# One core, fused attention and feed-forward over 64 sequences: the pieces of the software pipeline put in another order

## What is computed

```python
# layer 0: cross attention to 77 context tokens, 16 heads of 8
scores = einsum('bhqd,bhkd->bhqk', q, k) / sqrt(8)
scores = clip(0.5 * scores * mask + 0.5 * scores, -50, 50)
x = layernorm(x + softmax(scores) @ v @ Wo + bo) * gamma + beta
# layer 1: self attention, 16 heads of 64, rotary, causal within segments of 64 tokens,
# every query also sees 16 equal memory keys and 16 persistent keys
xn = rms_norm(x);  q, k, v = split(xn @ to_qkv_w);  q, k = rope(q), rope(k)
x = x + softmax(q @ [k_mem, k_pm, k].T / 8, masked) @ [v_mem, pm, v] @ to_out_w
a, g = split(rms_norm(x) @ ff_w1 + ff_b1);  x = x + silu(g) * a @ ff_w2 + ff_b2
```

## Time and profile before

| | us |
|---|---|
| median of 3 runs (lowest to highest) | 1216.44 (1213.78 to 1217.11) |
| profiled execution, its own time | 1214.23 |
| its span, first to last instruction | 1212.4 |
| busy: PE / PE weight loads / DVE / ACT / POOL | 1163.1 / 1019.5 / 987.0 / 1009.3 / 993.7 |
| mean granted TensorE clock, share of full | 0.996 |

### The profile page before, as it was taken

How to read it: one execution, slowest core, us unless ns; L and a number is a source line. 1 busy time by engine, 2 the same in 40 slices (tenths; PEclk the granted TensorE clock), 3 DMA queues, 4 the chain that set the end, 5 groups by cost and what they waited for, 6 DMA issues and landing times.

```text
span 1212.4 us, 54784 instructions
## 1 busy us (share of the span) xinstructions
PE 1163.1 (96%) x20707; PEld 1019.5 (84%) x20707; DVE 987.0 (81%) x2574; ACT 1009.3 (83%) x3341; POOL 993.7 (82%) x1678
## 2 busy tenths in 40 slices
PE   3799999999999999999999999999999999999985
PEld 2588888888888888888888888888888888888874
DVE  5578888888888888888888888888888888888872
ACT  1488888888888888888888888888888888888874
POOL 1578988888888888888888888888888888888874
PEclk9999999999999999999999999999999999999999
DMA  8122222222232223222222222322222222222220
GB/s 222 59 99 90 84 98 87 82 98 100 69 102 100 80 87 102 86 83 98 87 82 98 91 78 100 102 71 96 102 82 87 98 87 82 98 87 82 99 82 28
DMA packets 54344, 110.43 MB, mean 91 GB/s; under 512 B 9557, under 2 KB 28586, under 8 KB 54186
## 3 DMA queue, kind: packets, MB, share of 16 engines
q1 hardware_dynamic: 54314, 110.01, 27.7%
HBM read 21.63 MB, written 4.46 MB: 22 GB/s over the span
## 4 chain that ended last, share of the span: by engine, by line
PE 91%; DVE 3%; ACT 2%; DMA 1%; issue 1%; POOL 1%; SPq 0%; POOLq 0%; ACTq 0%; DVEq 0%
PE psum L968 18%; PE psum L1042 9%; PE psum L990 7%; PE psum L1023 7%; PE psum L975 6%; PE psum L1010 6%; PE psum L981 5%; PE psum L998 5%; PE psum L1111 4%; PE psum L961 3%; PE psum L1016 3%; PE psum L963 2%; PE psum L1127 2%; PE psum L962 2%; PE psum L999 2%; PE psum L1145 2%
## 5 line engine op out<-in xcount | busy, mean ns | idle before, releaser
L626 ACT ACTIVATE probs<-psum,less_max 128x81 f32<-128x81 f32 x1024 | 236.9, 343 | 50.8 <-DVE less_max L810 50.8
L968 PE MATMUL psum<-xnT,wqkv 128*128 128x128 f32 x2048 | 252.3, 277 | 0.9 <-ACT xnT L583 0.5
L968 PEld LDWEIGHTS psum<-xnT,wqkv 128*128 128x128 f32 x2048 | 240.3, 193 | 1.5 <-DVE z L806 0.7
L505 POOL TENSOR_TENSOR probs_near<-probs,rden 128x256 f32<-128x256 f32 x256 | 157.3, 614 | 71.9 <-DVE rden L894 71.9
L796 DVE TENSOR_TENSOR ra<-psum,rope 128x512 f32<-128x512 f32 x256 | 174.7, 682 | 12.9 <-PE psum L968 5.9
L497 POOL TENSOR_TENSOR kall<-ra,rs 128x512 f32<-128x512 f32 x128 | 162.8, 1272 | 21.2 <-DMA rs<-rb 9.7
L796 DVE TENSOR_TENSOR rb<-psum,rope 128x512 f32<-128x512 f32 x256 | 174.0, 680 | 0.0
L806 DVE TENSOR_TENSOR z<-psum,wT 77x512 f32<-77x512 f32 x256 | 163.7, 679 | 8.4 <-PE psum L975 2.5
L495 POOL TENSOR_TENSOR qT<-ra,rs 128x512 f32<-128x512 f32 x128 | 162.9, 1273 | 0.0
L501 POOL TENSOR_SCALAR z<-z 77x512 f32<-77x512 f32 x256 | 151.6, 609 | 7.9 <-DVE z L806 7.9
L652 ACT ACTIVATE z<-z 77x512 f32<-77x512 f32 x256 | 141.4, 648 | 8.7 <-POOL z L501 8.7
(11 more groups left out here) (135 smaller groups left out, 2887.7 us busy)
## 6 DMA issues: line engine op xcount, KB each, us to landing
rs<-rb SPq DMA_DIRECT2D x256, 256.0 KB, 2.3
vals_far<-vals SPq DMA_DIRECT2D x128, 128.0 KB, 2.3
seq_in<-in SPq DMA_DIRECT2D x64, 230.5 KB, 2.6
out<-out_sb SPq DMA_DIRECT2D x64, 64.0 KB, 1.6
ctx_all<-in SPq DMA_DIRECT2D x5, 320.0 KB, 9.4
wqkv<-in SPq DMA_DIRECT2D x1, 1536.0 KB, 14.0
vals_pre<-memv_dram SPq DMA_DIRECT2D x64, 4.0 KB
ctx_all<-in SPq DMA_DIRECT2D x3, 288.0 KB, 7.1
```

Source lines behind the costliest of these rows:

```text
L505: nc.gpsimd.tensor_tensor(probs_near[:, slots, :], probs[:, slots, 0:SEG], scale.broadcast_to([S, 4, SEG]), ALU.mult)
L626: last = nc.scalar.activation(probs[:, 4 * t + n, :], at(f"scores{t}")[:, KEYS * n:KEYS * (n + 1)], ACT.Exp, bias=less_max[:, 4 * t + n:4 ...
L968: last = mm(at(name)[:, S * n:S * (n + 1)], wqkv[:, lo + 128 * n:lo + 128 * (n + 1)], xnT[:], start=n == 0)
```

## The change

The instructions are the same; their order is new on all five engines, and so are the banks. Some pieces move over the border of a turn: `weigh` stood near the end of the turn and stands at its start, as work for `seq[2]`. On PE a turn now reads: c0T, weigh, scores(1), lin, wo, out, cross scores, scores(0), v0, v1, xnT, down, q1, hnT, k1, turn(3), q0, gate, k0, weigh_cross, turn(1), turn(2), pv, turn(0), qkv. Before it read: c0T, scores(1), wo, out, v0, cross scores, v1, scores(0), xnT, lin, hnT, k1, q1, k0, turn(2), turn(3), q0, weigh_cross, turn(1), down, turn(0), gate, pv, weigh, qkv.

```diff
         tasks = (
-            ("c0T", 0, 4, (c0T_ready,)),
-            ("wo", 3, 4, (y_ready,)),
-            ("out", 1, 2, (x1_ready,)),
-            ("v0", 0, 3, (vals0_ready,)),
-            ("xs0", 5, 5, (z0_masked,)),
-            ("xs1", 4, 5, (z1_masked,)),
-            ("xs2", 1, 5, (z2_masked,)),
-            ("xs3", 6, 5, (z3_masked,)),
...
+            ("out", 4, 2, (x1_ready,)),
+            ("scores1", 0, 3, (probs1_exp,)),
+            ("xs0", 1, 5, (z0_masked,)),
+            ("xs1", 3, 5, (z1_masked,)),
+            ("xs2", 2, 5, (z2_masked,)),
+            ("xs3", 7, 5, (z3_masked,)),
...
             def body(n, seq, done):
...
-                if seq[3] is not None:
-                    summed("q1").then_inc(q1_summed, 1)
                 if seq[1] is not None:
-                    wait(pool, out_ready, done[1])
-                    nc.gpsimd.tensor_tensor(x1b[:], x1[:], b2_rep[:], ALU.add).then_inc(x1b_ready, 1)
                     pool.wait_ge(gate_ready, done[2])
                     passed(pool, pool_passed)
                     nc.gpsimd.tensor_scalar(tanh_gate[:], tanh_gate[:], 1.0, 1.0, ALU.mult, ALU.add).then_inc(gate_raised, 1)
+                if seq[3] is not None:
+                    pool.wait_ge(swapped1_in, done[4] * 32)
+                    summed("q1")
+                    summed("k1").then_inc(k1_summed, 1)
+                if seq[1] is not None:
                     pool.wait_ge(gate_raised, done[2])
                     nc.gpsimd.tensor_tensor(ug[:], tanh_gate[:], half_gate[:], ALU.mult).then_inc(silu_ready, 1)
...
                 if seq[3] is not None:
                     pool.wait_ge(rden1_set, done[4])
                     normalised(1).then_inc(probs1_ready, 1)
+                    pool.wait_ge(rden2_set, done[4])
+                    normalised(2).then_inc(probs2_ready, 1)
                     pool.wait_ge(rden0_set, done[4])
                     normalised(0).then_inc(probs0_ready, 1)
...
             def body(n, seq, done):
                 if seq[4] is not None:
                     free(pe, "c0T", n)
+                    pe.wait_ge(c0_ready, done[5])
                     nc.tensor.transpose(at("c0T")[:, 0:S], c0[:], ident[:]).then_inc(c0T_filled, 1)
-                if seq[3] is not None:
-                    pe.wait_ge(mask2_set, done[4])
-                    pe.wait_ge(q1_summed, done[4])
+                if seq[2] is not None:
+                    if first(seq[2]):
+                        pe.wait_ge(w_in, WEIGHTS_IN)
+                    free(pe, "o0", n)
+                    free(pe, "o1", n)
+                    free(pe, "o2", n)
+                    free(pe, "o3", n)
+                    pe.wait_ge(memv_in, done[3] * 16)
+                    pe.wait_ge(vals_far0_in, done[3] * 16)
+                    pe.wait_ge(vals_far1_in, done[3] * 16)
+                    passed(pe, pe_passed)
+                    weigh().then_inc(heads_filled, 1)
+                if seq[3] is not None:
+                    pe.wait_ge(k1_summed, done[4])
+                    pe.wait_ge(mask3_set, done[4])
                     passed(pe, pe_passed)
                     scores(1).then_inc(scores1_filled, 1)
```

More of the change, by code:

```diff
@@ L39 @@
 CHUNKS = 4
[L40 removed]
+MEANS, POOLED, TOKENS_A, TOKENS_B = 4, 4, 4, 7
 LEAD = 6
@@ L466, in body @@
                         context_loads(0, 1)
+                if seq[4] is not None:
+                    sp.wait_ge(k1_rotated, done[5])
+                    passed(sp, sp_passed)
+                    for odd in range(2):
+                        sp.dma_start(rs[odd::2, half(1)], rb[1 - odd::2, half(1)]).then_inc(swapped1_in, 16)
             pipeline(sp, body)
@@ L519, in body @@
                 if seq[3] is not None:
+                    pool.wait_ge(xnT_hi_ready, done[4])
+                    nc.gpsimd.tensor_tensor(xnT_lo[:], xnT[:], xnT_hi[:].bitcast(F32), ALU.subtract)
+                    if first(seq[3]):
+                        value_weight_rest()
                     pool.wait_ge(swapped0_in, done[4] * 32)
                     summed("k0")
+                    summed("q0").then_inc(q0_summed, 1)
                 if seq[4] is not None:
@@ L849, in body @@
                     V.tensor_scalar(st0[:, 2:3], st0[:, 1:2], LN_EPS, None, ALU.add).then_inc(var0_ready, 1)
+                if seq[2] is not None:
+                    dve.wait_ge(out_filled, done[3])
+                    V.tensor_tensor(x1[:], at("out")[:, 0:D], y_keep[:], ALU.add).then_inc(x1_ready, 1)
+                if seq[4] is not None:
+                    if first(seq[4]):
+                        normalised_means()
                     dve.wait_ge(var0_ready, done[5])
@@ L1069, in body @@
                 if seq[1] is not None:
-                    free(pe, "lin", n)
-                    into_ff("lin", 0).then_inc(lin_filled, 1)
+                    free(pe, "down", n)
+                    pe.wait_ge(sT_ready, done[2])
+                    for i in range(FCH):
+                        last = mm(at("down")[:, 0:D], sT[0:FROWS[i], i, :], w2[0:FROWS[i], i, :], start=i == 0, stop=i == FCH - 1)
+                    last.then_inc(down_filled, 1)
+                if seq[4] is not None:
+                    if first(seq[4]):
+                        pooled_tokens()
+                    free(pe, "q1", n)
+                    project_turned("q1").then_inc(q1_filled, 1)
                 if seq[2] is not None:
@@ L1107, in body @@
                     turn(1).then_inc(turned1_filled, 1)
-                if seq[1] is not None:
-                    free(pe, "down", n)
-                    for i in range(FCH):
-                        last = mm(at("down")[:, 0:D], sT[0:FROWS[i], i, :], w2[0:FROWS[i], i, :], start=i == 0, stop=i == FCH - 1)
-                    last.then_inc(down_filled, 1)
-                if seq[3] is not None:
-                    free(pe, "turned0", n)
-                    pe.wait_ge(probs0_ready, done[4])
-                    turn(0).then_inc(turned0_filled, 1)
-                if seq[2] is not None:
-                    free(pe, "gate", n)
-                    pe.wait_ge(hnT_ready, done[3])
-                    into_ff("gate", 1).then_inc(gate_filled, 1)
+                    free(pe, "turned2", n)
+                    pe.wait_ge(probs2_ready, done[4])
+                    turn(2).then_inc(turned2_filled, 1)
                 if seq[5] is not None:
-                    if first(seq[4]):
-                        memory_tokens()
                     free(pe, "pv", n)
```

369 lines of the change are left out of this document (172 added, 197 removed).

## The result

The changed kernel takes 1247.06 us in the median of four runs (1242.32 to 1249.54), the kernel before on the same chip 1216.78: a ratio of **1.0241, 95% interval 1.0196 to 1.0287**. It is slower, as forecast, but by 30 us instead of 6, and outside the range. The profiled execution took 1242.32 us, its span is 1240.5.

The account below looks back on a forecast made before the run. A closed loop through the engines was to bind: eleven terms sum to 18.00 us a turn against 17.93. Over 60 turns +4.2 us, +1.7 at the end, giving 1220.1 on the profiled execution and 1222.3 us forecast; range 1203 to 1236.

Parts of the forecast that it names:

- The sign: Whole kernel: slightly slower was likeliest, chance 0.46; no difference 0.31, faster 0.23.
- Its own sign of a wrong mechanism: PE at scores(1): starting with the k1 sum long done would show the mechanism wrong.
- The forecast's loop, 18.00: Through PE, ACT, DVE and POOL, closed by k1's sum releasing scores(1): at least 18.00 us a turn.
- A second way round the same loop has nearly the same length: Last normalisation via turn(0), ACT's copy and weighing to scores(1): 3.30 us, against 3.38 on POOL.
- Can start 0.51 us after such a copy: PE's weighing after ACT's copy of turn(0): starts 0.51 us later (605.23 to 605.74), with seven semaphores.
- Shortening one of the two would not help: POOL's way (3.38 us) and the ACT way (3.30) to scores(1): nearly level, so shortening one gains nothing.
- PE alone, 17.27 to 17.49: PE's own work per turn: 17.93 less 0.40 and 0.26 gives 17.27, at most 17.49, say 17.4 us.
- The joined stretches: Weighing with scores(1), cross scores with scores(0): save 0.40 us a turn; inner shape changes cost 0 to 0.11, twice.
- The wait for x1: PE ahead of the cross scores: 0.26 us a turn, to be covered once it moves to v0.
- The instructions of start-up are the same: Start-up: instructions unchanged, no time added for it in the forecast's sum.
- The end: Last sequence: its weighing, 1.72 us, lies one turn later and adds 1.7 us.
- far slower: Cross scores' bank xs1 free late, PE waits every turn; each 0.1 us costs 6 us; inside the 0.46.

Follow-up runs that it names:

- h2: g1 with ACT's keep(3) moved behind the copy of u and wT's copy behind keep(0); turn 17.97 us, ratio 1.0115.
- g1: Changed kernel with three of weigh's seven waits left out and three of the other four moved ahead of c0's transpose; turn 17.97 us, ratio 1.0120.
- i1: h2 with POOL raising tanh_gate behind the sums of q1 and k1; turn 17.85 us, ratio 1.0066.
- g3: Changed kernel with DVE's context totals ahead of the wait for qkv and memory_tokens() behind u's matmuls and copy; turn 18.26 us, ratio 1.0222.
- e2: Changed kernel with POOL raising tanh_gate behind the sums of q1 and k1; turn 18.28 us, ratio 1.0249.
- e3: Changed kernel with six of weigh's waits moved ahead of c0's transpose on PE; turn 18.18 us, ratio 1.0216.

## Why the prediction was right or wrong

- **The sign: right, but in part by luck.** The forecast held that other engines would come to bind, and they did. Its own loop would have cost 0.04 us a turn (17.97 against 17.93), 2 us in all; the loss of 30 us came from a loop that it had put below that one, and from the start-up, which it had put at nothing. Its own sign of a wrong mechanism was scores(1) starting with the sum of k1 long done; it started 0.46 us behind it.
- **The forecast's loop, 18.00: right in size, but not the longest.** With the longer one lifted it measured 17.97 (h2). Its handover to scores(1) was 0.14 us (taken: 0.20), and POOL's term from the first of three normalisations to the end of k1's sum 5.65 (611.78 to 617.43 in h2; taken: 5.67).
- **"A second way round the same loop has nearly the same length": the step that failed.** It put this way at 3.30 us where POOL's has 3.38, so the loop over it at 17.92. It let turn(0) start 0.05 us behind the last normalisation and summed turn(0), 0.49, keep(0), 0.48, and 0.51 to weighing. In the trace turn(0) starts at 622.42, 0.36 us behind the normalisation's end (622.06), since it stands behind `pv`, and `pv` waits for u_kept at the end of ACT's row. From the normalisation's end to weighing it is 1.83 us (623.89 in the next turn; 605.63 is the same place one turn earlier), where the step had 0.10 + 0.49 + 0.48 + 0.51 = 1.58. These 0.25 us bring 17.92 to 18.17. The other 0.09 is spread over the terms: from scores(1) to the normalisation's end 14.72 (607.34 to 622.06; taken: 14.62), with xnT the largest (614.21 to 615.05, 0.84; taken: 0.76). ACT's row, 8 us without a gap, was never followed; of ACT only single copies had been read.
- **"Can start 0.51 us after such a copy": misread in the rows of before.** PE was not waiting for that copy, but busy with `pv`, which starts 0.02 us ahead of the copy's end:
```profile
605.21 0.60 PE L1127 MATMUL psum<-cross_w,u 128*128 128x128 f32 x4
```
  Weighing at 605.74 follows its four transposes at PE's own pace. The size came out near the handover of the changed kernel by luck. There it was mostly the price of seven waits: 0.45 with seven, at most 0.14 with one (g1).
- **"Shortening one of the two would not help": half right.** The ACT side stood 0.29 us above the POOL side, and shortening it alone gave all of that (g1). From 17.97 on it was right: h2, which shortens the ACT side further, gained nothing.
- **PE alone, 17.27 to 17.49: slightly low.** i1 takes 17.85 with three waits left in it, turn(2) for POOL (0.17) and about 0.05 in front of each of turn(0) and xnT: near 17.6, an estimate. The joined stretches save no exit in their middle: from weighing's last part to scores(1) it is 0.62 us, as it was before to the qkv matmul, and from the cross scores to scores(0) 1.04, as before to full-size work. So the upper value was the better one. The rule that the forecast cited agrees (the Trainium skill, TensorEngine Tiling (Array Packing), Tiling Modes). The wait for x1 did go.
- **"The instructions of start-up are the same": true, and worth nothing.** Their place in the order cost 6 us (g3): DVE's 5.4 us of totals and the memory tokens came to stand in the chain that leads to c0's second transpose. The end cost 1.7 by forecast; the last interval between two of c0's transposes grew by 2.5 (17.1 to 19.5).
- **The rival "far slower"** (bank xs1 late) did not occur: the cross scores follow `out` directly (609.06 to 610.94, 1.88 us from start to start).
- **The range** covered the errors of the terms of one loop, but had no case for another loop above it.

## What to carry to other kernels

In a software pipeline in which several engines are about 80% busy, a new order can close a loop through each of them. Look for an engine's row without a gap that ends in a signal PE needs, and add up every such loop; the longest decides, and shortening the second gains nothing until the first is gone (e2 and i1 make the same edit: 0 and 0.12 us a turn). When a signal comes last, put the other waits ahead of it or leave out those that are implied, and check which waits follow a moved instruction: its bank's last reader too. Steps of the start-up that sit inside the first turns need placing like any other.

## What was not expected of the hardware

- Waits that are already satisfied cost PE time when they stand behind a signal that comes late. Seven waits put 0.45 us between keep(0)'s end and the first matmul, one wait 0.14 at most. In the kernel before, where no signal is late there, two waits fewer and four moved ahead changed nothing (b1, 0.9994, interval 0.9983 to 1.0006). Moved in front of another piece that follows closely they delay that one (e3: 0.19 us at c0's transpose).
- The profile calls the idle time in front of weighing "issue", 0.25 us a turn, with no engine's name; it was 15 us in the whole.
